# A decoder layer in one program: the first norm moved behind a second, turned copy of x, and three norms that begin from ScalarE's exp(-ln/2)

## What is computed

```python
x = x + attention(_layernorm(x))          # 16 heads of 32, Wq Wk Wv Wff bff
x = x + cross_attention(ctx, ctx, _layernorm(x))   # one head of 512
x = x + ffn(_layernorm(x))                # scores against 2048 keys, top 8, a gate, h + gate * sum

def _layernorm(x, axis=-1, eps=1e-05):
    m = jnp.mean(x, axis=axis, keepdims=True)
    v = jnp.var(x, axis=axis, keepdims=True)
    return (x - m) / jnp.sqrt(v + eps)
```

## Time and profile before

| | before |
|---|---|
| median of 3 runs | 2862.33 us |
| the profiled execution, its time | 2859.07 us |
| its span, first to last instruction | 2857.2 us |
| PE busy | 2649.0 us (93%), 18042 matmuls |
| DVE busy | 2104.9 us (74%), 4071 instructions |
| ACT busy | 1421.1 us (50%), 4214 |
| POOL busy | 785.7 us (27%) |
| mean granted TensorE clock | 0.973 |
| chain that ended last, by engine | PE 90%, DVE 2%, DMA 2%, issue 2% |
| DMA | mean 110 GB/s |

### The profile page before, as it was taken

The page is one execution under the profiler, slowest core; times in us unless marked ns, Lnnn a source line. Parts: engine busy times, 40 slices in busy tenths (PEclk is TensorE's granted clock), DMA queues, the critical chain, the costliest instruction groups (busy, mean ns, idle before and its releaser), DMA issues.

```text
span 2857.2 us, 53958 instructions
## 1 busy us (share of the span) xinstructions
PE 2649.0 (93%) x18042; PEld 1983.5 (69%) x18042; DVE 2104.9 (74%) x4071; ACT 1421.1 (50%) x4214; POOL 785.7 (27%) x651
## 2 busy tenths in 40 slices
PE   6899999999999999999999999999999999999830
PEld 4667777777777777777777777777777777777610
DVE  4446778878777788877777878777788877777652
ACT  2345554445455444555554445455544455555343
POOL 0001323222223232222323222223232222233245
PEclk9999999999999999999999999999999999999965
DMA  5112323333333332333323333333332333333799
GB/s 167 57 57 76 103 91 118 103 102 105 107 101 100 102 120 86 108 107 109 103 91 116 110 96 104 107 101 104 99 120 89 107 107 110 101 93 108 180 237 181
DMA packets 102683, 313.05 MB, mean 110 GB/s; under 512 B 14577, under 2 KB 15089, under 8 KB 94417
## 3 DMA queue, kind: packets, MB, share of 16 engines
q1 hardware_dynamic: 54002, 180.37, 19.2%
q0 software_dynamic: 48640, 132.16, 17.4%
HBM read 269.35 MB, written 43.12 MB: 109 GB/s over the span
## 4 chain that ended last, share of the span: by engine, by line
PE 90%; issue 2%; DVE 2%; DMA 2%; ACT 1%; POOL 1%; SPq 1%; POOLq 0%; DVEq 0%; ACTq 0%
PE psX L985 45%; PE psA L985 19%; PE psF L985 8%; PE psA L994 8%; PE psA L1072 4%; PE psA L1049 4%; PE psX L994 3%; DMA vg<-in_L_ffn_aux_values,idx 1%; DVE xT_lo L775 1%; PE psF L994 1%; ACT xT_hi L567 1%; POOL out L540 1%; POOL vg L523 0%; SPq L371 0%; ACT paT L550 0%
## 5 line engine op out<-in xcount | busy, mean ns | idle before, releaser
L523 POOL DMA_INDIRECT vg<-in_L_ffn_aux_values,idx x512 | 516.5, 1009 | 1635.1 <-DVE agg L890 830.9
L586 ACT ACTIVATE pa<-psA,nmax 112x224 f32<-112x224 f32 x1024 | 443.6, 449 | 150.3 <-DVE nmax L794 147.6
L890 DVE SCALAR_TENSOR_TENSOR agg<-vg,wt,agg 112x512 f32<-112x512 f32 x420 | 367.5, 875 | 16.2 <-DMA vg<-in_L_ffn_aux_values,idx 2.9
L794 DVE TENSOR_REDUCE nmax<-psA 112x4 f32<-112x896 f32 x256 | 266.7, 1083 | 149.8 <-PE psA L1049 149.8
L985 PE MATMUL psX<-big,gT 128*112 128x375 f32 x1024 | 333.4, 478 | 1.3 <-ACT nx L622 1.0
L985 PE MATMUL psX<-pT,cx 125*128 125x224 f32 x1536 | 307.5, 357 | 0.0
L550 ACT COPY paT<-psA 112x448 f32<-112x448 f32 x512 | 236.5, 544 | 111.1 <-PE psA L994 108.7
L985 PEld LDWEIGHTS psX<-pT,cx 125*128 125x128 f32 x1536 | 285.5, 190 | 7.7 <-issue 0.3
L807 DVE TENSOR_TENSOR pa<-pa,rsum 112x896 f32<-112x896 f32 x256 | 279.5, 1092 | 8.8
L985 PEld LDWEIGHTS psX<-big,gT 128*112 128x112 f32 x1024 | 177.4, 176 | 127.1 <-ACT nx L622 1.2
L985 PE MATMUL psX<-m,xnxT 128*112 128x512 f32 x512 | 235.6, 603 | 0.0
(11 more groups left out here) (195 smaller groups left out, 5301.5 us busy)
## 6 DMA issues: line engine op xcount, KB each, us to landing
big<-in_ctx_t SPq DMA_DIRECT2D x32, 1500.0 KB, 6.7
cx<-in_ctx SPq DMA_DIRECT2D x32, 1500.0 KB
xa<-in_x SPq DMA_DIRECT2D x32, 448.0 KB, 4.7
xr<-in_x SPq DMA_DIRECT2D x32, 448.0 KB, 3.9
out<-x SPq DMA_DIRECT2D x32, 448.0 KB, 3.1
agg_scratch<-agg SPq DMA_DIRECT2D x60, 224.0 KB, 6.4
vg<-in_L_ffn_aux_values,idx POOLq DMA_INDIRECT x512, 3.7
over_weights<-agg_scratch SPq DMA_DIRECT2D x15, 448.0 KB, 13.5
```

The costliest lines, as they stand in the source:

```text
L523: pool.indirect_dma_start(vg[:, c % SLOTS, k, :], None, aux_values, bass.IndirectOffsetOnAxis(ap=idx[:, t, n:n + 1], axis=0))\
L586: last = nc.scalar.activation(pa[:, t, h, :], psA[0:R, h, t * S:(t + 1) * S], ACT.Exp, bias=nmax[:, k % 2, h, t:t + 1], accum_out=rsum[:, ...
L794: nc.vector.tensor_reduce(nmax[:, k % 2, h:h + 2, :], psA[0:R, h:h + 2, 0:T * S].rearrange("p h (t s) -> p h t s", t=T), AX_X, ALU.max, ne ...
L890: last = nc.vector.scalar_tensor_tensor(dst, vg[:, c % SLOTS, k, :], w, dst, ALU.mult, ALU.add)
```

## The change

Four things change.

1. The first norm is done otherwise. A new step ("N", "norm"), one batch ahead, only takes the statistics of the rows in `xa` and stores mean and 1/sqrt (448 numbers, `moments`) to a scratch tensor in DRAM. ("N", "spread") reads them back into all 128 partitions (`spread`). x is also given to the kernel turned (`in_x_t`, arranged on the host like the turned context that was there before), loaded into `centered`, and ("N", "center") subtracts the mean and multiplies by 1/sqrt on VectorE over 128x896 numbers, then ScalarE rounds (`xT_hi`) and VectorE takes the rest (`xT_lo`). The 8 transposes are gone.
2. All three norms take their first guess from ScalarE: Ln of `ve`, then Exp with scale -0.5 (`guess_rstd`), and VectorE waits for it and does one Newton step in place of three.
3. The v products go in halves of 256 columns through 4 fills, where there were 2 fills of 512, so that the count of fills stays a multiple of the 4 banks.
4. ORDER is another table. The loop now runs over iterations 3 to 29, with 30 unrolled, and the setup steps stand elsewhere (FIRST and SETUP).

```diff
 ORDER = (
-    ("A", "norm", 0), ("X", "enter", 0), ("A", "turn", 0), ("G", "sum", 0), ("X", "norm", 0), ("A", "qk", 0),
...
+    ("A", "qk", 0), ("G", "sum", 0), ("G", "sum", 1), ("X", "enter", 0), ("X", "norm", 0), ("A", "value", 0),
...
-FILLS = {("A", "turn"): 2, ("A", "qk"): 1, ("A", "value"): 2, ("A", "score"): HB, ("A", "prob"): 2 * T,
+FILLS = {("A", "qk"): 1, ("A", "value"): 2 * T, ("A", "score"): HB, ("A", "prob"): 2 * T,
...
+FIRST = (("N", "norm", 0), ("N", "spread", 0), ("W", "split", 0), ("N", "center", 0), ("W", "split", 1),
+         ("W", "split", 2), ("W", "keys", 0), ("W", "keys", 1), ("W", "keys", 2), ("W", "keys", 3))
...
             sp.dma_start(xa[:, :, :], tiles(row(x, 0))).then_inc(x_loaded, 16)
+            sp.dma_start(flat(centered), row(x_t, 0)).then_inc(xt_loaded, 16)
...
+            def store_moments(b, _):
+                sp.wait_ge(moments_ready, b + 1)
+                with nc.allow_non_contiguous_dma(reason="448 numbers"):
+                    sp.dma_start(row(moments_dram, b).rearrange("k r -> r k"),
+                                 moments[:, :, :].rearrange("p k t -> p (k t)")).then_inc(moments_stored, 16)
...
+            def spread_moments(b, _):
+                sp.wait_ge(moments_stored, 16 * (b + 1))
+                wait(sp, xt_scaled, b)
+                sp.dma_start(flat(spread), row(moments_dram, b).rearrange("k r -> (k r)").partition_broadcast(P))\
+                    .then_inc(moments_spread, 16)
...
+            def center_hi(b, _):
+
+                act.wait_ge(xt_scaled, b + 1)
+                wait_full(act, "A", max(FILL["A", "value", 0] + 2 * T - 1, FILL["A", "qk", NB - 1]), b - 1)
+                nc.scalar.copy(xT[0][:, :, :], centered[:, :, :]).then_inc(xT_hi, 1)
...
+            def guess_rstd(s):
+
+                def step(b, _):
+                    act.wait_ge(steps[s], VE_STEP + per_batch[s] * b)
+                    nc.scalar.activation(rstd[s][:, :], ve[s][:, :], ACT.Ln).then_inc(log_taken[s], 1)
+                    act.wait_ge(log_taken[s], b + 1)
+                    nc.scalar.activation(rstd[s][:, :], rstd[s][:, :], ACT.Exp, scale=-0.5).then_inc(rstd_guessed[s], 1)
+                return step
...
-                mark(s, nc.vector.tensor_scalar(rstd[s][:, :].bitcast(I32), ve[s][:, :].bitcast(I32), -0.5, RSQRT_SEED,
-                                                ALU.mult, ALU.add))
-                for _ in range(3):
...
+                dve.wait_ge(rstd_guessed[s], b + 1)
+                mark(s, nc.vector.scalar_tensor_tensor(tmp[s][:, :], rstd, -0.5, ve[s][:, :], ALU.mult, ALU.mult))
...
+            def center_scaled(b):
+                mean, rstd = (spread[:, k, :].unsqueeze(1).to_broadcast([P, C, S]) for k in range(2))
+                xt = centered[:, :, :]
+                dve.wait_ge(xt_loaded, 16 * (b + 1))
+                dve.wait_ge(moments_spread, 16 * (b + 1))
+                nc.vector.tensor_tensor(xt, xt, mean, ALU.subtract).then_inc(mean_taken, 1)
+                dve.wait_ge(mean_taken, b + 1)
+                nc.vector.tensor_tensor(xt, xt, rstd, ALU.mult).then_inc(xt_scaled, 1)
...
+                for t in range(T):
+                    for half in range(2):
+                        j, cols = FILL["A", "value", 0] + 2 * t + half, slice(half * D // 2, (half + 1) * D // 2)
+                        wait_free(pe, "A", j, b)
+                        filled("A", j, product3(bank("A", j)[0:R, 0:D // 2],
+                                                [(both(xT, ALL, c, slice(t * R, (t + 1) * R)), both(wvT, ALL, c, cols))
+                                                 for c in range(C)]))
```

More of the change, by code:

```diff
@@ L162, in build @@
         xa = sb("xa", [R, T, D])
+        moments = sb("moments", [R, 2, T])
+        spread = sb("spread", [P, 2, S])
+        centered = sb("centered", [P, C, S])
         xT = (sb("xT_hi", [P, C, S], F32R), sb("xT_lo", [P, C, S], F32R))
@@ L302, in iteration @@
                         step[s, name](b, arg)
+            for s, name, arg in FIRST:
+                if (s, name) in step:
+                    step[s, name](0, arg)
             for i in range(3):
                 iteration(i)
-            with eng.Fori(3, B - 1) as i:
+            with eng.Fori(3, B - 2) as i:
                 iteration(i)
+            iteration(B - 2)
             iteration(B - 1)
@@ L478, in _ @@
                           ("W", "cb"): first_cxT, ("W", "gb"): first_ctx,
-                          ("X", "score"): next_cxT, ("X", "mix"): next_ctx, ("A", "turn"): next_x, ("X", "enter"): next_xr,
+                          ("X", "score"): next_cxT, ("X", "mix"): next_ctx, ("N", "norm"): store_moments,
+                          ("N", "spread"): spread_moments, ("N", "center"): next_xt, ("X", "enter"): next_xr,
                           ("F", "norm"): store_base,
@@ L690, in _ @@
             pipeline(act, {("Z", "log"): log_var, ("Z", "gate"): logits, ("Z", "scale"): scale,
-                           ("W", "split"): split_hi, ("A", "turn"): turn_hi, ("A", "mix"): mixed,
+                           ("W", "split"): split_hi, ("N", "center"): center_hi, ("N", "norm"): guess_rstd("N"),
+                           ("X", "norm"): guess_rstd("X"), ("F", "norm"): guess_rstd("F"), ("A", "mix"): mixed,
                            ("A", "qk"): qk, ("A", "value"): value, ("A", "score"): exp_scores, ("A", "prob"): probs_turned,
@@ L709, in settle, with statistics @@
                 dve.wait_ge(steps[s], per_batch[s] * b + count[s])
-            per_batch = {"A": A_STEPS, "X": X_STEPS, "F": F_STEPS, "G": G_STEPS}
-            def norm(s, b, src, dst, normed):
+            def statistics(s, b, src, rstd):
                 count[s] = 0
@@ L740, in norm, with x_moments @@
                 last.then_inc(normed, 1)
-            def a_norm(b, _):
+            def x_moments(b, _):
                 dve.wait_ge(x_loaded, 16 * (b + 1))
-                norm("A", b, xa, xa, xa_normed)
+                statistics("N", b, xa, rstd["N"][:, :])
+                assert count["N"] == N_STEPS
+                wait(dve, moments_stored, 16 * b)
+                nc.vector.tensor_copy(moments[:, 0, :], mv["N"][:, :, 0])
+                nc.vector.tensor_copy(moments[:, 1, :], rstd["N"][:, :]).then_inc(moments_ready, 1)
             def x_norm(b, _):
@@ L798, in share @@
             def share(b, k):
+                if k == 0:
+                    count["A"] = 0
                 for t in range(T):
@@ L971, in _ @@
                            ("W", "gb"): made_gb,
-                           ("A", "norm"): a_norm, ("A", "turn"): turn_lo, ("A", "qk"): qk,
+                           ("N", "norm"): x_moments, ("N", "center"): center_lo, ("A", "qk"): qk,
                            ("A", "score"): maxima, ("A", "share"): share,
@@ L1033, in value @@
                     pe.wait_ge(split, 3 * C)
[L1034 removed]
+                pe.wait_ge(xT_split, b + 1)
                 for t in range(T):
[L1036 to L1039 removed]
+                    for half in range(2):
+                        j, cols = FILL["A", "value", 0] + 2 * t + half, slice(half * D // 2, (half + 1) * D // 2)
[3 more added lines that the diff above has]
+                                                 for c in range(C)]))
             def scores(b, k):
```

132 lines of the change are left out of this document (69 added, 63 removed), and 24 rows, old and new, of tables (ORDER, SETUP).

## The result

The changed kernel takes **3133.18 us** (median of 4 runs, 3126.75 to 3135.56), the kernel before, run beside it, 2863.77 (4 runs, 2860.9 to 2866.07). The ratio is 1.0938, 95% interval 1.0917 to 1.0958. The forecast was 2916 with a range that ended at 2965. The direction is right, the time is not, by 217 us.

A forecast was written before the change was run, and what follows sets the result against it. TensorE was taken as the bound. Iterations 3 to 31 at +1.5 us gave 43.5, the start +10 and the end +3.5: +57 on 2859.07, 2916 us, with a range of 2838 to 2965.

The forecast's parts named there:

- +1.5 us, 83.8 in all: One loop iteration: TensorE's saving of 1.9 us against waits of 1.4, 0.8, 0.4 and 0.8.
- More gets late than I see: Rival, in the loop: another step or the slower values hold, +2.7 an iteration, 2950 to 2965 us; chance 0.13.
- the clock gives nothing to win in the loop: TensorE in a middle iteration: granted clock already 1.00, busy 80.87 of 82.30 us.
- The guess at X, 3.06 us: ScalarE's part of a norm: two table loads of 1.28 us each, and 0.5 for both small activations.
- the rival with one load: Norms: one table load serves Ln and Exp, a guess costs 1.8 us, 2818 us in all; chance 0.04.
- The four small waits in TensorE: Waits an iteration at X turn 1.4 us, A prob 0 0.8, F turn 0.4, X prob 0 0.6.
- Two loads for each norm, no drain: ScalarE in each norm: two table loads of 1.28 us, and no drain around them.
- The rival built on it (3140): Each table load costs ScalarE twice its row, each guess 2.6 us longer, about 3140 us; chance 0.03.
- G sum 2 beside GpSimd's bias: Ahead of A share 0: the weighted sum takes 3.36 us beside the bias, 1.53 elsewhere; TensorE waits 0.8 at prob 0.
- The start: Before the first product: moments stored and read back, 9.4 us, then centering and split; product near 37, +10 (bounds 5 and 16).
- my first term: TensorE's saving: A's turn and wait go, 2.41 us, v costs 0.5 more; net -1.9 us an iteration.
- TensorE gets its whole 1.9 back: Rival, in the loop: the guess is cheap or covered throughout, 2812 us, faster; chance 0.15.

The follow-up runs named there:

- The exchange of two steps: The changed kernel with G sum 6 moved from in front of A share 2 to behind it: 3022.01 us, ratio 1.0561.
- the nearly empty load: The changed kernel, its own order, loading only 8 of the turned context's 3000 columns from the second batch on: 3022.02 us, ratio 1.0548.
- the best order: Changed kernel with G sum 6 behind A share 2, G sum 2 behind A score 0: 2844.91 us with VectorE's guess, 3001.39 with ScalarE's.

## Why the prediction was wrong, point by point

- **The step that failed is a wait put at nothing:** the walk goes from X prob 0 to N center, and its sum, "+1.5 us, 83.8 in all", has no term for A prob 2. It takes every weighted sum as VectorE work only. A weighted sum also needs its gathers, and the new order puts sum 6 ahead of share 2, and its gathers behind the store of the moments and a 1500 KB load. TensorE waits 4.1 us an iteration there and loses 2.5 more at the lower clock, some 190 of the 217 us in 29 iterations. "More gets late than I see" had the kind of this at 2.7 us, two fifths of its size. The exchange of two steps and the nearly empty load each give back 111 of it, and the exchange gives 173 where the guess is gone as well.
- **"the clock gives nothing to win in the loop"** was true of the kernel before and silent on what the clock could cost. The 1.00 of the earlier trace rows was granted with one wait of 1.43 us in 82. Behind a wait of 4.10 us it reads 0.53 to 0.60 in every iteration, behind several waits of 0.3 to 1.1 in some iterations and not in others. It is over half of the reason why 111 and 90 make 262 together; the rest is waits that take each other's place.
- **The guess at X, 3.06 us, was mis-sized:** it is 1.86, by chance what the rival with one load has (1.8), though two loads run. ScalarE's timeline at the next X norm, the first load and what follows:

```profile
1580.64 1.28 ACT L710 ACT_TABLE_LOAD   x1
1589.77 0.20 ACT L710 ACTIVATE rstd_X<-ve_X 112x2 f32<-112x2 f32 x1 [7.85 <-DVE ve_X L772]
1590.00 1.28 ACT L712 ACT_TABLE_LOAD   x1
1591.29 0.20 ACT L712 ACTIVATE rstd_X<-rstd_X 112x2 f32<-112x2 f32 x1
```

  The first load ran 9 us ahead of the activation it serves; the wait for `ve` holds the activation alone. With 1.86 in its place the walk would have had a wait of 0.2 at X turn. It is 0.68, as VectorE's last add of X enter begins at 1496.12, 0.6 us behind the start of v and not 0.1. Where ScalarE is busy until `ve` is ready, both loads count, with what stands ahead of them. VectorE's waits for the three guesses, in total, times, longest:

```profile
DVE tmp_N L776 <- ACT rstd_N L712: 125.5, 32, 4.1
...
DVE tmp_F L776 <- ACT rstd_F L712: 94.2, 32, 3.8
DVE tmp_X L776 <- ACT rstd_X L712: 59.6, 32, 1.9
```

- **The four small waits in TensorE were right in place, and three of them nearly in size:** X turn 0.68 (1.4), prob 0 0.71 (0.8), F turn 0.3 (0.4), X prob 0 0.77 (0.6), F learn and what is behind it more than forecast. The price of the guess was too low all the same: the walk gives it 2.6 us an iteration (1.4, 0.4 and 0.8), and in the best order it is 156 us, 5.2 an iteration. The larger part of that is further waits (F learn, A mix 1, A prob 2, and X prob 0 at 1.11), a smaller one slower steps; with F's guess back on VectorE the other two norms still cost 90 us at a full clock.
- **Two loads for each norm, no drain:** right. 1.28, then 0.20, with 0.01 between. The Trainium skill's page "ScalarE: Activation LUTs" has a drain of some 1.38 us for each load, which does not appear in any of these rows, and one set for Ln and Exp, which this program does not get. The rival built on it (3140) comes near the measured time by accident: its mechanism is refuted by the rows above and by the exchange of two steps that takes 111 us away without touching a load.
- **G sum 2 beside GpSimd's bias:** right, and shown. Moved away from share 0 it gave 26 us, for 20 expected, and the wait at prob 0 went with it. VectorE's sum and GpSimd's bias in the changed kernel, each longer than in the earlier trace rows:

```profile
1502.26 3.54 DVE L950 SCALAR_TENSOR_TENSOR agg<-vg,wt,agg 112x512 f32<-112x512 f32 x2
```

```profile
1502.42 2.83 POOL L547 TENSOR_TENSOR x<-x,cb 112x1024 f32<-112x1024 f32 x1 [3.71 <-DVE nx L786]
```

- **v:** nearly right. The products follow each other every 0.12 us for a forecast of 0.127; the 6.28 us from its start holds 0.43 that X enter had before, so it cost 0.3 us more than the 512s, for 0.5 forecast. **N center:** covered, as forecast.
- **The start,** "+10": the first product is at 42.80 us, +16.5, past the upper bound of 16 of which it was given. "Store and reading back 9.4", twice the 4.7 us of a small load, was too little: the store was issued at 21.96, the reading back could be issued only at 30.96, and centering began at 36.03, so they took 9.0 and 5.1 us, 14.1 together. Centering, cast, remainder and split then took 6.8 for the 6.7 forecast, and the first product is this row:

```profile
42.80 0.56 PE L1046 MATMUL psA<-xT_hi,wqT_hi 128*128 128x224 f32 x1 [17.43 <-DVE wkT_lo L969]
```

  And the loss grows behind it. The first X enter, before and after, is 32 us later:

```profile
113.60 7.09 PE L985 MATMUL psX<-wffT,oT 128*112 128x512 f32 x16 [0.56 <-ACT oT L550]
145.57 7.61 PE L1046 MATMUL psX<-wffT,oT 128*112 128x512 f32 x16
```

  In between the q/k product of batch 0 takes 5.12 us for 2.75 (TensorE had stood idle 17.4), and more steps run at a lower clock behind waits. From there to the last X enter the kernel loses 240 us, for 43.5 forecast, and behind it 0.3, for 3.5.

- **Parts 1, 3 and 4 can pay.** Without the guess and with two sums moved, the period is 80.72 us for 82.3: 1.6 of the 1.9 us of my first term. Its first X enter is still 30 us late, so of what the loop gains 16 us are left. The rival "TensorE gets its whole 1.9 back" needed all of the other costs to be absent.

## What to carry to other kernels

When an order is rewritten, walk each step's inputs that come by DMA as well as its engine time: where its transfer is now issued, behind which load and which store of small pieces, and how soon the result is due. On a kernel whose bound engine has no gaps, price a long new wait with the slower stretch behind it, and test fixes together as well as alone: here they paid more together. Work taken off an engine that is not the bound was worth nothing here, and its stand-in on a second engine delayed copies that had no part in it.

## What the runs showed of the hardware

- Gathers of 112 rows, issued 2.5 and 3.7 us behind a store of 448 numbers of four bytes and 1.2 and 2.5 us behind a load of 1500 KB on another queue, were waited for until 14.2 and 13.0 us after issue. Without the store, in the kernel before, two gathers 3.3 and 4.5 us behind such a load landed after 3.6 and 4.1 us. Loads behind the store took 10.3 us (448 KB) and 14.8 us (1500 KB) where they took 4.7 and 6.7, with the DMA engines 85% busy at 42 GB/s for 7 us. In the run with the guess on VectorE the gathers were issued 0.6 us behind the large load and VectorE waited 3.8 to 4.2 us for them.
- A table load on ScalarE is not held by the wait of the activation behind it (load at 1580.64, activation at 1589.77).
- The granted clock of TensorE sank from 1.00 to 0.60 and 0.53 around a wait of 4.10 us. In the run with the best order and the guess it read 0.84 and 0.90 behind waits of 0.47 and 1.11 us, in some 17 of 28 iterations, and in the run with F's guess on VectorE, with waits of 0.73, 0.68, 0.55 and 1.03 an iteration, 1.00, as in the kernel before with one of 1.43.
- 448 numbers stored four bytes at a time took 9.0 us before they could be read back, and 15.8 us when the store was issued among the first loads of weights.
